# Delta rule of a decoder: queries, keys, norms and values computed beside the spike scan, one square root and one reciprocal for all units

## The reference, cut to what matters

```python
h = silu(conv)                                   # [B, T, 128]
q = (h @ wq).reshape(B, T, H, DK); k = (h @ wk).reshape(B, T, H, DK)
v = (h @ wv).reshape(B, T, H, DV)
q = q / (norm(q, axis=-1) + EPS); k = k / (norm(k, axis=-1) + EPS)
sd = (h @ w_spike).reshape(B, T, H, DK)
ab = (silu(h @ w_au + b_au) @ w_ad + b_ad).reshape(B, T, H, DK)
bb = h @ w_beta + b_beta
def step(carry, inp):                            # over the tokens
    mem = DECAY * mem + sdt
    hard = (mem > THR); spike = hard             # forward value
    mem = mem - spike * THR
    alpha = sigmoid(abt + alpha_spike * spike)
    beta = sigmoid(bbt + sum(spike * beta_spike, axis=-1))
    active = sum(hard, axis=-1) > 0
    alpha = where(active, alpha, 1); beta = beta * active
    s = s * alpha[..., None]
    u = einsum('bhd,bhdv->bhv', kt, s)
    s = s - beta * outer(kt, u) + beta * outer(kt, vt)
    out = einsum('bhdv,bhd->bhv', s, qt)
```

## Time and profile before

| | |
|---|---|
| median of 3 runs | 7280.35 us (7275.85 to 7287.11) |
| the profiled execution's own time | 7309.51 us |
| its span | 7307.6 us |
| PE, DVE, ACT, POOL busy | 77%, 68%, 45%, 28% |
| spike stage, scan and all | 3225.8 to 3466.9 us of the span |
| prepare stage | 3468.0 to about 3891 us |

### The profile page before, as it was taken

One profiled execution on the slowest core, in us unless ns is written; L12 is line 12 of the kernel. 1 busy time (PEld: TensorE's weight loads), 2 busy tenths in 40 slices (PEclk: granted clock), 3 DMA queues, 4 the chain that ended last, 5 costly groups with the idle time before them and its releaser, 6 DMA issues. The chain is left out here.

```text
span 7307.6 us, 135138 instructions
## 1 busy us (share of the span) xinstructions
PE 5607.2 (77%) x43987; PEld 3111.2 (43%) x43987; DVE 4967.0 (68%) x8964; ACT 3317.2 (45%) x4792; POOL 2010.7 (28%) x2592
## 2 busy tenths in 40 slices
PE   3786647688888839950787999997666699999759
PEld 1343435222222224420555999996534333333334
DVE  5564663799999944457896666663544599999654
ACT  0233424466666712220783444443223377777512
POOL 1101324566766720000004555551313200000000
PEclk6898878799999969975997999897787799999979
DMA  2220016222222210000233434342204422222200
GB/s 59 49 44 9 6 31 211 76 56 58 56 58 57 50 37 10 0 2 3 115 125 115 122 110 126 107 117 64 75 6 158 133 66 64 63 65 65 60 11 12
DMA packets 756225, 484.32 MB, mean 66 GB/s; under 512 B 484248, under 2 KB 682753, under 8 KB 754369
## 3 DMA queue, kind: packets, MB, share of 16 engines
q1 hardware_dynamic: 755904, 480.05, 23.2%
HBM read 282.34 MB, written 196.37 MB: 66 GB/s over the span
## 5 line engine op out<-in xcount | busy, mean ns | idle before, releaser
L1481 ACT ACTIVATE c0a_raised<-c0a_sb 128x1024 f32<-128x1024 f32 (+1 forms) x832 | 837.3, 1025 | 320.5 <-PE c0a_sb L1293 316.2
L1246 POOL TENSOR_SCALAR c0a_prob<-c0a_raised 128x1024 f32<-128x1024 f32 (+1 forms) x832 | 866.1, 1041 | 395.1 <-ACT c0a_raised L1481 363.5
L1481 ACT ACTIVATE c1a_prob<-c1a_sb 128x1024 f32<-128x1024 f32 (+1 forms) x832 | 828.9, 1029 | 205.6 <-PE c1a_sb L1293 202.0
L1369 DVE TENSOR_REDUCE c0a_pmax<-c0a_sa 128x2 f32<-128x802 f32 (+1 forms) x704 | 697.2, 990 | 86.3 <-PE c0a_sa L1261 81.9
L1369 DVE TENSOR_REDUCE c1a_pmax<-c1a_sa 128x2 f32<-128x802 f32 (+1 forms) x704 | 698.3, 992 | 70.7 <-PE c1a_sa L1261 66.7
L1261 PE MATMUL c0a_sa<-c0a_K,c0a_Q 48*128 48x401 bf16 (+1 forms) x2048 | 479.4, 354 | 196.8 <-DVE c0a_pmax L1369 101.5
L1261 PE MATMUL c1a_sa<-c1a_K,c1a_Q 48*128 48x401 bf16 (+1 forms) x2048 | 466.2, 346 | 103.4 <-DVE c1a_pmax L1369 47.7
L1312 PE MATMUL c0a_pv<-c0a_prob,c0a_V 128*9 128x256 f32 x6656 | 533.9, 392 | 4.8 <-POOL c0a_prob L1246 4.1
L1312 PE MATMUL c1a_pv<-c1a_prob,c1a_V 128*9 128x256 f32 x6656 | 519.4, 383 | 0.7 <-issue 0.5
L1261 PEld LDWEIGHTS c0a_sa<-c0a_K,c0a_Q 48*128 48x128 bf16 x2048 | 131.1, 94 | 688.6 <-DVE c0a_pmax L1369 330.9
L3092 DVE COPY_PREDICATED dd_AB<-dd_keys_mask,dd_lb 128x512 f32<-128x512 int32 x320 | 286.7, 959 | 156.2 <-PE dd_lb L2915 142.2
(11 more groups left out here) (595 smaller groups left out, 12068.0 us busy)
## 6 DMA issues: line engine op xcount, KB each, us to landing
unit_in<-dp_res SPq DMA_DIRECT2D x64, 512.0 KB, 2.6
dd_src<-unit_in SPq DMA_DIRECT2D x64, 512.0 KB, 6.3
k_ctx<-c0k_parts SPq DMA_DIRECT2D x16, 1200.8 KB, 4.7
c0a_K<-k_ctx SPq DMA_DIRECT2D x128, 150.1 KB
k_ctx<-c1k_parts SPq DMA_DIRECT2D x16, 1200.8 KB, 4.7
c1a_K<-k_ctx SPq DMA_DIRECT2D x128, 150.1 KB
unit_v<-dp_vs SPq DMA_DIRECT2D x64, 256.0 KB, 2.8
dd_l_img<-dd_AB SPq DMA_DIRECT2D x64, 256.0 KB
```

What stands on the lines that cost most here:

```text
L1246: pool.tensor_scalar(prob[0:r, in_ring(v, c), :, :, :], raised[0:r, in_ring(v, c), :, :, :], 1.0, math.exp(-FLOOR), ALU.min, ALU.max).then ...
L1369: dve.tensor_reduce(pmax[:, u, :, 2 * pr + s, k], sa2[:, :, 0:w], AX.X, ALU.max).then_inc(a_reduced, 1)
L1481: act.activation(dst[0:r, in_ring(v, c), :, :, :], sb_[0:r, in_both(v, c), :, :, :], ACT.Exp).then_inc(b_exp, 1)
```

## The change

The queries, keys, norms and values move from the prepare stage into the spike stage, onto the engines that idle during the scan.

- The spike projection has two PSUM slots instead of four (and one for the hidden of alpha instead of two), since the new work needs PSUM too. All loads of the stage, now with the three weights wk, wq and wv, are waited for together.
- After it PE walks the 64 units once for the norms: keys and queries are projected, ACT squares them, and PE sums the squares of all units into one PSUM tile of 128 rows, row 2n+h for unit n and head h, by a shifted window of a 0/1 matrix `pick`. ACT takes one root of that tile.
- DVE stops its scan after 152 tokens (`TURN`), waits for the root, adds EPS and takes one reciprocal, then scans the other 104 tokens.
- SP stores the reciprocals to DRAM and loads them back for each unit, each of its two rows copied to 64 partitions. PE walks the units a second time (keys, queries, and now the values), ACT copies both out of PSUM, POOL multiplies keys and queries by the loaded scale, SP stores values and normalized keys and queries.
- The prepare stage keeps the gates: PE has 4 matmuls of a unit, ACT two sigmoids, DVE three instructions. SP loads the normalized key back from `unit_in`, POOL multiplies it by beta, SP stores alpha and key x beta. Of alpha's two last instructions one is left (`max` with the inactive flag instead of a product and a sum). Loops over the units are written out.

```diff
-        sdp = st.ps("sdp", [P, 4, C])
-        aup = st.ps("aup", [R_AU, 2, C])
+        sdp = st.ps("sdp", [P, 2, C])
+        aup = st.ps("aup", [R_AU, 1, C])
+        qk = st.ps("qk", [P, 2, 2, L])
+        ssq = st.ps("ssq", [P, 2, L])
+        vp = st.ps("vp", [P, 2, 2, 2 * DV])
...
+                def load_scale(n):
+                    if n >= RING:
+                        sp.wait_ge(normed, n - RING + 1)
+                    sp.dma_start(scale[:, n % RING, :, :], scale_img[2 * n:2 * n + 2].unsqueeze(1)
+                                 .to_broadcast([2, DK, 2, L])).then_inc(scale_loaded[n % RING], 16)
+
+                sp.wait_ge(inverted, 1)
+                sp.dma_start(scale_img, rcp[:, :, :]).then_inc(scale_stored, 16)
+                sp.wait_ge(scale_stored, 16)
+                for n in range(RING - 1):
+                    load_scale(n)
+                for n in range(U):
+                    u = n % 2
+                    if n + RING - 1 < U:
+                        load_scale(n + RING - 1)
+                    sp.wait_ge(v_copied, n + 1)
+                    sp.dma_start(unit_v[n], vs[:, u, :, :]).then_inc(v_stored[u], 16)
+                    sp.wait_ge(normed, n + 1)
+                    sp.dma_start(unit_in[n][:, 0:2, :], res[:, u, :, :]).then_inc(in_stored[u], 16)
...
+                        if i >= 2:
+                            pe.wait_ge(doubled, i - 1)
...
+                def square_sum(n):
+                    pe.wait_ge(squared, n + 1)
+                    pe.matmul(ssq[:, :, :].rearrange("p c t -> p (c t)"), pick[:, P - 2 - 2 * n:2 * P - 2 - 2 * n],
+                              sq[:, n % 2, :, :].rearrange("p c t -> p (c t)"), start=(n == 0), stop=(n == U - 1),
+                              skip_group_check=True).then_inc(ssq_ready, 1)
...
+                for n in range(U):
+                    if n >= 2:
+                        pe.wait_ge(squared, n - 1)
+                    project(n)
+                    if n >= 1:
+                        square_sum(n - 1)
+                square_sum(U - 1)
...
+                act.activation(nrm[:, :, :], ssq[:, :, :], ACT.Sqrt).then_inc(rooted, 1)
...
+                for n in range(U):
+                    u = n % 2
+                    pool.wait_ge(qk_copied, n + 1)
+                    pool.wait_ge(scale_loaded[n % RING], 16 * (n // RING + 1))
+                    if n >= 2:
+                        pool.wait_ge(in_stored[u], 16 * (n // 2))
+                    pool.tensor_tensor(res[:, u, :, :], raw[:, u, :, :], scale[:, n % RING, :, :], ALU.mult
+                                       ).then_inc(normed, 1)
...
-                with dve.Fori(1, L // STEP) as g:
+                with dve.Fori(1, TURN // STEP) as g:
+                    for k in range(STEP):
+                        token(g * STEP + k, k)
+                dve.wait_ge(rooted, 1)
+                dve.tensor_scalar(nrm[:, :, :], nrm[:, :, :], EPS, None, ALU.add).then_inc(eps_added, 1)
+                dve.wait_ge(eps_added, 1)
+                dve.reciprocal(rcp[:, :, :], nrm[:, :, :]).then_inc(inverted, 1)
+                with dve.Fori(TURN // STEP, L // STEP) as g:
...
+                    if n >= 2:
+                        pe.wait_ge(za_ready, n - 1)
+                        pe.wait_ge(b0_ready, n - 1)
+                        pe.wait_ge(alpha_ready, n - 1)
+                        pe.wait_ge(b1_ready, n - 1)
...
+                def gates(n):
+                    u = n % 2
...
+                    dve.scalar_tensor_tensor(res[:, n % 4, 0, :], cnt[:, u, 0:L], 0.5, a0[:, u, :], ALU.is_lt, ALU.max
+                                             ).then_inc(alpha_ready, 1)
...
+                for n in range(U):
...
+                    dve.scalar_tensor_tensor(za[:, u, :], hard[:, h, b * L:(b + 1) * L], asp[:, h:h + 1],
+                                             ab[:, u, 0, 0:L], ALU.mult, ALU.add).then_inc(za_ready, 1)
+                    if n >= 1:
+                        gates(n - 1)
+                gates(U - 1)
```

More of the change, by code:

```diff
@@ L2327, in spike_stage @@
     STEP = 8
+    EPS = 1e-6
+    U = B * PAIRS_H
+    TURN = 152
+    RING = 4
+    scale_img = nc.dram_tensor(f"{name}_scale_img", [P, 2, L], F32, kind="Internal").ap()
     with Stage(nc, name) as st:
@@ L2517, in _ @@
                 pe.wait_ge(spread_ready, 2)
[L2519 to L2530 removed]
+                for n in range(U):
+                    b, h = divmod(n, PAIRS_H)
+                    u = n % 2
@@ L2548, in unit @@
-                    if h == 0:
-                        pe.wait_ge(hs_ready, b + 1)
-                    if not early(n, 1) and not (isinstance(b, int) and h == 0):
-                        pe.wait_ge(v_copied, n)
-                    for s in range(2):
-                        ins = pe.matmul(vp[:, s, :], hs[:, s, :], wv[:, 2 * h * DV:2 * (h + 1) * DV],
-                                        start=True, stop=True)
-                    ins.then_inc(v_projected, 1)
-                units(pe, unit)
+                    pe.matmul(cnt[:, u, 0:L], same[:, :], hard[:, h, cols], start=True, stop=True).then_inc(counted, 1)
```

286 lines of the change are left out of this document (140 added, 146 removed).

## The result

| | us, median (lowest to highest) | ratio to before, 95% interval |
|---|---|---|
| before | 7283.73 (7275.85 to 7289.84) | |
| changed | 7463.66 (7451.94 to 7477.96) | 1.0252 (1.0236 to 1.0268) |

A forecast was written before the change was run, and what follows sets the result against it. DVE was taken to bound both stages: alone in the scan, busiest in prepare. Hiding work beside the scan and shortening the second stage moves the delta stage from 3893.2 to 3768.4, -124.8 us: median 7280.35 - 125 = 7155 us, range 7110 to 7205.

The forecast's parts named there:

- Start of the scan: Spike stage: more loads to await add 3.7 us, two PSUM slots 2 us; scan starts at 3273.2 instead of 3267.5.
- First walk and turn: Spike stage: PE 1.72 us a unit, 110 us for 64; root 2 us before DVE's turn; 3.9 us stay on DVE.
- Second walk: Spike stage, from POOL's start at 3396.2: 2.2 us a unit, 141 us, ending at 3537.0.
- the landing (2.6 for twice the bytes): Second walk: time until a 256 KB store of a normalized unit has landed, taken as 2.6 us from a 512 KB store.
- The ring: Second walk: `res` has two slots, so POOL(n+2) waits for store(n) to land; 4.3 to 4.4 us for two units.
- The bound of 4.1 us: Second walk: upper bound of the store's landing, from another 512 KB load; gives 2.9 us a unit.
- Bytes as the other bound: Second walk: 768 KB of transfers a unit at about 400 GB/s take 1.9 us, below the ring's 2.2.
- The *slower* rival: Second walk: slow store landings in the two-slot ring; slower than before from 6.9 us, 7337 us at 8.7; chance 3%.
- What it does to the scan: Second walk: POOL's product holds DVE's scan, 1.5 tokens a cycle against 3 without POOL; DVE ends at 3547.4.
- "3477 + 9": End of DVE's scan by itself plus the comparison, said to be hidden only because the walk is as long.
- Second stage: Prepare stage: loop between PE and DVE, 3.1 us a unit, 198.4 us for 64; delta stage starts at 3768.4.
- "Nothing outside it is touched": Whole kernel: only the stretch from the first load to the delta stage, 667.4 us before, changes; all other stages stay.

The follow-up runs named there:

- B: Theory that 64 reads of one row are slow; tested on the changed kernel with scale loads of the same shape from different rows: 7499.31 us.
- place 217: Changed kernel with scale load as two transfers, PE's gate wait moved to the count product, and 192 do-nothing waits in PE's second stage: 7239.37 us.
- place 224: Kernel before, with 632 products of 8 columns added to PE's program in the spike stage: 7365.45 us, ratio 1.0106.
- place 121: Changed kernel with scale load as two transfers and PE's gate wait moved to the count product, without padding: 7161.93 us, ratio 0.9846.

## Why the prediction was wrong

- *Start of the scan:* right. PE's first weights 7.4 us after the stage's start (forecast 6.9), the scan 48.0 us after it (47.4).
- *First walk and turn:* right. 1.72 us a unit at clock 1.00, root 2.3 us early, turn after 113.9 us of scan (113.2), 3.8 us for both instructions.
- *Second walk:* this is the step that failed, and in it the term "the landing (2.6 for twice the bytes)". The ring was right, product and signals were right; the landing was 9.9. The price was taken from stores, which the walk's own stores resemble, as if they had the engines to themselves. The load between them was priced at its landing alone (2.5 for 128 KB) and at its share of the total bytes, and both rows came from transfers with another shape. With the loads gone the walk took 2.15 us a unit. The bound of 4.1 us was far from holding. (The formula of the Trainium skill (DMA: Bandwidth & Descriptors, "Anatomy of one DMA") that the prediction sets beside this, 2.0 us and bytes over 436 GB/s, is fitted there to transfers that GpSimd issues. SP's 256 KB stores here landed in 2.1 us with no loads beside them, and in 3.6 and 9.9 with the load as two transfers and as one.)
- *Bytes as the other bound:* "768 KB at about 400 GB/s, 1.9 us" was too fast: 298 GB/s at a share of 0.91, so 2.6 us. With the walk repaired this alone would have cost 27 us of the forecast gain.
- The *slower* rival had the place and nearly the price: the ring around store landings, deciding from 6.9 us, 5.2 us a unit and 7337 us at 8.7. It got 3% because the rows against it were those of transfers of another shape, and its own guess at the cause, reads of the same rows, was the wrong one (B). A rule that was at hand had named the right one: the Trainium skill (DMA: Bandwidth & Descriptors, "Why a DMA increments its semaphore by 16 and not by 1") says that a transfer is split over the largest number of engines, at most 16, that divides the slowest dimension of both sides. That is 2 for this load, 16 for each of the two loads, and the traces agree: 2 packets in flight, then 14 to 17. It was not weighed.
- *What it does to the scan:* right in mechanism and size (1.55 tokens a cycle for 1.5, and the stretch gone when POOL reads nothing). It cost nothing in the changed kernel, since the walk was 2.9 times as long as forecast. Beside it stands a slip of the prediction: alone, 104 tokens from 3390.2 on end at 3467.7, and the comparison at 3476.6; the 3477 already holds the comparison, so "3477 + 9" and the 3486 count it twice. The sum does not use them.
- *Second stage:* right, 221.5 us from its start to the delta stage's, forecast 218.1; 3.17 us a unit for 3.1.
- *"Nothing outside it is touched":* wrong. The instructions that the change adds moved a later loop across a block of code, which cost 33 to 82 us in the profiled executions of the changed kernel and its variants. No row of the trace of before could give that price, but its position is a thing that the change alters, and the sum held no term for it.

The forecast and the measurement of the two stages differ by 266.8 us. The walk explains it: 407.5 us (3383.8 to the issue of the last store at 3791.3) for 141. What remains cancels to within a microsecond: POOL's start 3.7 late, start and turn together 1.3 late, the second stage 3.4 longer, and 8.4 less between the walk's end and the next stage, where forecast DVE was to be late.

## What to carry to other kernels

Before pricing a transfer by its bytes, look at its slowest dimension on both sides: a broadcast of two rows to 2 x 64 partitions ran on 2 of 16 engines and held every other transfer of the walk to its pace; two transfers of 64 partitions each moved the same bytes 2.4 times as fast. When no engine is the limit and the DMA share is low as well, count the packets in flight before looking at the queue. And when a change writes loops out, compare the untouched loops behind it too: a wait named "issue" of some microseconds that returns once a pass is code being fetched, and shifting the code by the right part of a 16 KB block took it away here (by three other amounts it did not).

## What the hardware showed that was not expected

- Issuing a transfer can itself block: the first four loads held SP 9.18 us, and in the steady walk the store of the values 2.7 to 3.2 us each. With the load in two transfers the same store is issued in 0.59 us (median), though the transfers are at a share of 0.91 there, so it goes with the load in one transfer and not with busy engines as such. With these loads on ACT's queue it is ACT that is held, 6.15 us in the median for one issue, while SP issues its stores in 0.32: the queue that has the loads holds its issuer. Why it does isn't shown.
- The granted clock fell to 0.59 in the slow walk, where PE had, in every 6.45 us, the products that the first walk's clock of 1.00 would do in 1.7; they took twice as long (170.89 us of the 310), without consequence.
- Each stall for code brought nine packets of 16 KB, over the whole pass, and a pass without a stall none.
- The stalls for code have sharp edges: at place 217 the stage takes 1245.9 us, at place 224 it takes 1131.5. The places rest on counts of trace records: all of PE's records taken together give 65, 119, 152, 184, 216 and 255 in place of 67, 121, 153, 185, 217 and 1, with 0 and 224 as they are. That is two or less from the table, and it changes neither the order nor the two stretches. Why at place 121 only some passes stall, and a different number in each execution, stays open.
